# A grouped-query layer whose second up half is made in the query bank

## The reference, cut to what matters

```
h, kv   = rmsnorm(x, ln1), rmsnorm(ctx, ln1)
q, k, v = rope(h @ Wq), rope(kv @ Wk), kv @ Wv        # 16 query heads, 4 key and value heads, 64 wide
attn    = softmax(q @ k.T / 8 + mask) @ v
hidden  = x + attn @ Wo
y       = rmsnorm(hidden, ln2)
out     = hidden + (silu(y @ Wgate) * (y @ Wup)) @ Wdown   # 1024 wide in the middle
```

## Time and profile before

| | |
|---|---|
| time, median of 3 runs | 1357.92 us (1354.81 to 1359.65) |
| time of the profiled execution | 1358.02 us |
| span of the profiled execution | 1356.2 us |
| mean granted TensorE clock | 0.943 |
| PE busy | 1219.7 us, 90% of the span |
| DVE busy | 728.2 us, 54% |
| ACT busy | 610.4 us, 45% |
| POOL busy | 428.3 us, 32% |

### The profile page before, as it was taken

One profiled execution on the slowest core, in us unless ns is written; L12 is line 12 of the kernel. 1 busy time (PEld: TensorE's weight loads), 2 busy tenths in 40 slices (PEclk: granted clock), 3 DMA queues, 4 the chain that ended last, 5 costly groups with the idle time before them and its releaser, 6 DMA issues.

```text
span 1356.2 us, 36206 instructions
## 1 busy us (share of the span) xinstructions
PE 1219.7 (90%) x14778; PEld 1028.2 (76%) x14778; DVE 728.2 (54%) x1656; ACT 610.4 (45%) x1464; POOL 428.3 (32%) x545
## 2 busy tenths in 40 slices
PE   4899999977899999999778869999999999998986
PEld 2566666655599999999567759889889888876665
DVE  5688787667322000000466457657656657636776
ACT  2455555422444544545222235445445445535542
POOL 3224446153323222226200134424424423332200
PEclk9999999876899999999866879999999999999998
DMA  9000000000489999999510010100100100000000
GB/s 313 2 2 2 2 2 18 9 17 25 136 287 327 338 354 361 352 354 314 179 52 2 2 41 22 40 22 21 41 22 21 41 22 21 21 2 1 18 17 33
DMA packets 91572, 130.73 MB, mean 96 GB/s; under 512 B 13392, under 2 KB 74064, under 8 KB 91280
## 3 DMA queue, kind: packets, MB, share of 16 engines
q1 hardware_dynamic: 85360, 117.11, 26.0%
q0 software_dynamic: 4768, 10.26, 2.1%
q10 hardware_dynamic: 1280, 1.04, 0.2%
HBM read 116.82 MB, written 11.57 MB: 95 GB/s over the span
## 4 chain that ended last, share of the span: by engine, by line
PE 76%; DVE 11%; issue 4%; ACT 3%; DMA 3%; POOL 2%; SPq 1%; another core or an unknown queue 1%; ACTq 0%; DVEq 0%; POOLq 0%
PE scores L1776 9%; PE bank L1786 9%; PE scores L1470 8%; PE bank L2326 8%; PE bank L491 5%; PE bank L1470 4%; PE scores L508 4%; DVE reg L880 3%; PE scores L518 3%; PE bank L540 3%; PE scores L2316 3%; PE scores L2302 3%; PE bank L500 3%; PE bank L529 2%; PE scores L1978 2%
## 5 line engine op out<-in xcount | busy, mean ns | idle before, releaser
L1821 ACT ACTIVATE w_ca<-scores,fc1b 128x128 f32<-128x128 f32 x312 | 114.1, 367 | 139.3 <-PE scores L1776 117.2
L1776 PEld LDWEIGHTS scores<-reg 128*128 128x128 f32 x1248 | 145.2, 192 | 7.0 <-issue 2.5
L1776 PE MATMUL scores<-reg 128*128 128x128 f32 x1248 | 146.3, 275 | 3.8 <-DMA reg<-in_fc 1.2
L880 DVE TENSOR_REDUCE reg<-scores 128x8 f32<-128x1024 f32 x96 | 113.0, 1220 | 64.2 <-PE scores L508 55.6
L2396 ACT ACTIVATE reg<-reg,mx 128x128 f32<-128x128 f32 x256 | 99.3, 389 | 106.8 <-DVE mx L2547 106.8
L1855 DVE TENSOR_TENSOR reg<-bank,reg 128x256 f32<-128x256 f32 x39 | 16.6, 425 | 240.9 <-PE bank L1786 225.5
L1786 PE MATMUL bank<-reg,w_ca 128*128 128x256 f32 x624 | 141.1, 379 | 0.3 <-DVE small L1846 0.3
L1786 PEld LDWEIGHTS bank<-reg,w_ca 128*128 128x128 f32 x624 | 115.6, 190 | 14.5 <-DVE small L1846 0.3
L1470 PEld LDWEIGHTS scores<-reg 128*128 128x128 f32 x1024 | 116.8, 192 | 1.9 <-ACT reg L2404 1.1
L1470 PE MATMUL scores<-reg 128*128 128x128 f32 x1024 | 117.0, 275 | 0.5 <-ACT reg L2404 0.5
L2326 PE MATMUL bank<-reg,w_ca 128*128 128x256 f32 x496 | 115.1, 385 | 0.0
(11 more groups left out here) (305 smaller groups left out, 2375.2 us busy)
## 6 DMA issues: line engine op xcount, KB each, us to landing
reg<-in_fc SPq DMA_DIRECT2D x78, 1024.0 KB
w_sa<-grouped_values SPq DMA_DIRECT2D x64, 128.0 KB, 2.6
reg<-expert_out SPq DMA_DIRECT2D x16, 256.0 KB, 3.5
xres<-in_x SPq DMA_DIRECT2D x4, 512.0 KB, 11.4
ctxr<-in_ctx SPq DMA_DIRECT2D x1, 2048.0 KB, 15.3
w_l<-in_w_l SPq DMA_DIRECT2D x2, 1024.0 KB, 13.0
routed_rows<-reg SPq DMA_DIRECT2D x8, 256.0 KB
grouped_values<-reg SPq DMA_DIRECT2D x16, 128.0 KB, 1.7
```

The costliest lines, as they stand in the source:

```text
L880: ins = nc.vector.tensor_reduce(mxpad.rearrange("p (c n d) -> p n c d", c=C, d=DH)[:, 4 * half:4 * half + 4, :, 0], scores4[:, 2 * half:2 ...
L1776: ins = nc.tensor.matmul(S[n % 4][:, 0:P], up_w8[j % 2][:, c, f * P:(f + 1) * P], xbT[:, j % 2, c, :], start=(c == 0), stop=(c == C - 1))
L1821: nc.scalar.activation(h1[:, j % 2, f, :], S[n % 4][:, 0:P], ACT.Gelu, bias=fc1b[:, bass.ds(e * FC + f, 1)]).then_inc(M["fc1_free"], 1)
```

## The change

The job u1 of slots 1 to 14 (batches 0 to 13) gets home "c", bank 7, in which qb of the same slot stood before, in place of home 0. In slots 15 and 16 u1 stays in bank 0.

```diff
@@ -1405,6 +1405,8 @@
         for t in range(-2, B + 1):
             for name, ahead, home in SLOT_JOBS:
+                if name == "u1" and t < B - 1:
+                    home = "c"
                 if 0 <= t + ahead < B and (name, t + ahead) not in IN_TOP_TEN:
                     job_at[name, t + ahead] = (home, n_jobs[home])
                     n_jobs[home] += 1
```

## The result

The changed kernel takes 1344.83 us, median of 6 runs (1336.5 to 1347.67), against 1358.17 us for the kernel before (6 runs, 1354.81 to 1362.88): ratio 0.989, 95% interval 0.9853 to 0.9927. In a second job, beside the experiments, it was 0.9894 (0.9864 to 0.9924), 1340.53 against 1354.56 us; one of the 17 runs of the kernel before in that job was a slow one of 4118.13 us, and the ratio leaves it out. The forecast was 1342.7 us, faster; the range was 1340.0 to 1348.0 us.

A forecast was written before the change was run, and what follows sets the result against it. The prediction took each slot as TensorE's work plus a hole before the value products, held by the gate's release of bank 0. 15.4 - 0.1 = 15.3 us off 1358.02 us gave 1342.7 us, range 1340.0 to 1348.0 us.

The forecast's parts named there:

- (a): Value products, slots 1 to 14: the wait for the gate goes, 14.4 us, plus 1.0 us closer start; 15.4 us.
- rival 1: Before the products: hole closes only in part, reading seven semaphores costs something; 1344.5 or 1346.1 us; chance 0.25.
- (b): Down projection's wait for the gate, now beside the products: 1.0 us cover left, no cost; 0.1 us once in slot 13.
- (c): u1's new wait for bank 7, released by qb's second rope multiplication: u1 comes 3.7 us late for it, cost nothing.
- (d): Next slot's qb now waits for the gate in bank 7, but comes some 12 us later: cost nothing.
- (e): VectorE and ScalarE beside TensorE: gate overlapping the products costed at nothing; bound 0.69 us per slot, 9.7 us.
- Rival 2: Gain given back by slower products (1352.4 us) or another wait in the hole's place (near 1358); chance 0.07.
- the clock: Denser TensorE might be granted a lower clock; dense stretches had 1.00, so no case or chance of its own.

The follow-up runs named there:

- more_work_before: Kernel before plus three unused statistics of 512 columns ahead of the second gate in slots 1 to 12: slot 26.11 us against 25.47, pause 1.57 us.
- prep_behind: Kernel before with L3's preparation behind the second gate in slots 13 and 14: slot 13's pause 0.94 us, single total 1365.24 us.
- swapped: Kernel before with g1 and u1 exchanged, u1 in bank 3 and g1 in bank 0: slot 25.52 us, pause 0.98 us before the products.
- u1_in_t: Against the kernel before: u1 in bank 4 in all slots, L3's preparation behind the second gate: 1340.67 us, ratio 0.989.
- late_query_c: Changed kernel (u1 in bank 7) with query half b's rope multiplications behind the last transpose of the probabilities: slot 25.60 us, pause 0.88 us before u1.
- twice_more_after: Changed kernel plus six unused statistics ahead of the second gate in slots 1 to 12: slot 25.74 us, pause 1.22 us before the down projection.
- late_query_t: Changed kernel with query half b's rope multiplications behind the last transpose, but u1 in bank 4: slot 24.48 us, slots 1 to 15 344.15 us.

## Why the prediction was right

**The bound.** The reading that a slot is TensorE's work plus one hole held: with the hole closed, TensorE is busy 300.76 of 301.00 us.

**What held the products.** The chain's "issue" was the gate on VectorE. Shown three ways: work ahead of the gate lengthens the pause (more_work_before), taking work away from ahead of it shortens slot 13's (prep_behind), and the exchange of banks makes the profile name it (swapped). The distances of 0.20 to 0.21 us behind the gate's end, read in three slots, had been enough to infer it, and the 0.21 us came back when the gate was moved either way.

**(a) The size.** 15.4 us were forecast for the pauses and the closer start, 15.3 in all; 15.26 are measured. That they agree to 0.1 us is in part luck, since two small terms off in opposite directions nearly cancel: slot 13 cost 0.02 us and not 0.1, and the down projection follows the products' start by 2.03 us and not 2.02 in each of 14 slots, 0.14 us, which the sum had at nothing. The products start 0.07 us ahead of u1's modelled end, the value taken from the scores, so rival 1 (seven semaphores cost something when all are satisfied) is out. In u1_in_t, where slot 15's gate too is out of the products' way, they start there at the same 0.07 us. The rule of the Trainium skill that a change of tiling mode drains TensorE ("TensorEngine Tiling (Array Packing)", Tiling Modes) stands with the trace: 0.07 us into row tiles in each of the 14 slots, against 0.16 us between whole-array jobs (g1 and u1 too, which are whole-array jobs both). The traces show more than the prediction used: in the slots of L2, in every profile, each change between the whole array and row tiles, in either direction, leaves an overlap of 0.04 to 0.08 us where nothing is waited for, and each change between whole-array jobs one of 0.15 to 0.17 us. It isn't the number of semaphores: g0 behind the keys and values and the down projection behind the products both carry three, and have 0.16 and 0.07 us. That a drain is what takes the 0.09 us is the rule's reading; the ends are modelled.

**(b) The down projection.** Cover of 1.0 us in an ordinary slot: it was used up between three and six statistics, as it should be. The gate starts 0.04 us behind u1's modelled end, as was said. In slot 13 I had 0.1 us of wait; 0.02 us is measured (2.05 against 2.03 us from the products' start). The step that was off is the release: I carried the 0.21 us of the products over to the down projection, where it is 0.11 us.

**(c) The new wait.** 3.7 us early, nothing paid; what it costs if the cover goes is shown by late_query_c.

**(d) and (e).** No wait of qb for the gate, and of the 0.69 us that the products could have taken longer beside the gate, 0.01 to 0.02 us is measured (2.10 us). Rival 2 is out.

**What the prediction didn't have.** The 1.63 us of lower clock in slot 15. I gave the clock no case, because the stretches of rows 7 were dense and at 1.00, and slot 15 was to be as before. Neither stretch of rows 7 has slot 15 in it, where TensorE has waits of its own of 0.52, 1.26 and 0.47 us. But these waits don't explain the dip: the kernel before had them too (0.52, 1.27 and 0.47 us, the same 17.68 busy of 20.00 us) and kept 1.00. With the dip the sum comes to 1358.02 - 15.3 + 1.6 = 1344.3 us, beside the 1344.83 us measured. That this is so close is luck: the medians scatter by some us (the changed kernel's was 1340.53 us in the second job), and how often the timed runs had the dip isn't known.

## What to carry to other kernels

When a bank is shared in turns, look at who reads it last before the next writer and where that reader stands in its engine's order: the job before the widest claim belongs in a bank that the claim doesn't need. A repeated pause labelled "issue" can have a releaser all the same; a constant distance to one instruction's end, in slots where everything else has moved, names it. And each moved wait has a cover that can be counted in the timeline (here 3.7 us at u1 and 1.0 us at the down projection); a later change of VectorE's order can use it up.

## What the runs showed of the hardware

The distance from the end of a VectorE instruction to the start of the TensorE job that waited for it was not one number: 0.21 us for the products (seven semaphores), 0.25 us for them in swapped, 0.14 us for u1 in late_query_c (two semaphores) and 0.11 us for the down projection in twice_more_after (three), but 0.15 us for it in slot 13 of late_query_t. What sets it isn't shown. Semaphores that were all satisfied early cost TensorE nothing that shows: with seven (products), six (scores) and three (down projection) the job starts 0.06 to 0.08 us before the modelled end of the one ahead in an ordinary slot, across a change between row tiles and the whole array each time. In the two profiles that are looked at here, a stretch at a granted clock of 0.50 cost 1.6 us, in 64 matmuls of the whole array (9.04 against 7.41 us) or in the 128 of the products (3.66 against 2.09 us).
